# Cross-attention on one core: V's row halves moved behind the transposes, the first pair's scores in two PSUM banks of their own, the last step handled pair by pair

## What is computed

```python
h = _layernorm(x, gamma, beta)                       # x: (8, 256, 256)
Q = (h @ Wq).reshape(B, NQ, N_HEADS, HEAD_DIM)       # 16 heads of 64
K = (context @ Wk).reshape(B, NC, N_HEADS, HEAD_DIM) # context: (8, 256, 192)
V = (context @ Wv).reshape(B, NC, N_HEADS, HEAD_DIM)
attn = jnp.einsum('bihd,bjhd->bhij', Q, K)
attn = jax.nn.softmax(attn, axis=-1) * scale
vals = jnp.einsum('bhij,bjhd->bihd', attn, V).reshape(B, NQ, INNER)
out = vals @ Wo + bo
return x + out
```

## Time and profile before

| | |
|---|---|
| median of three runs | 330.03 us |
| the profiled execution's own time | 329.93 us |
| its span (first to last instruction) | 327.9 us |
| PE busy | 319.3 us, 97% |
| DVE and ACT busy | 253.1 us each, 77% |
| POOL busy | 155.2 us, 47% |
| share of PE in the chain that ended last | 93% |
| granted TensorE clock | full in every slice |

### The profile page before, as it was taken

The page is one execution under the profiler, slowest core; times in us unless marked ns, Lnnn a source line. Parts: engine busy times, 40 slices in busy tenths (PEclk is TensorE's granted clock), DMA queues, the critical chain, the costliest instruction groups (busy, mean ns, idle before and its releaser), DMA issues.

```text
span 327.9 us, 9688 instructions
## 1 busy us (share of the span) xinstructions
PE 319.3 (97%) x3771; PEld 280.9 (86%) x3771; DVE 253.1 (77%) x588; ACT 253.1 (77%) x798; POOL 155.2 (47%) x288
## 2 busy tenths in 40 slices
PE   5999999999999999999999999999999999999985
PEld 4879888899888889988889988889988888988874
DVE  5898787977778788787878778787777878767784
ACT  4899888877878877888777877787787887776862
POOL 5586578616644256433662336631664425233330
PEclk9999999999999999999999999999999999999999
DMA  6980000020001100020000200003000000000000
GB/s 181 262 256 4 0 2 3 2 91 2 2 1 54 37 3 0 2 90 2 3 3 3 88 2 2 2 1 91 2 2 2 32 3 2 2 3 32 2 3 32
DMA packets 10860, 10.70 MB, mean 33 GB/s; under 512 B 960, under 2 KB 10304, under 8 KB 10816
## 3 DMA queue, kind: packets, MB, share of 16 engines
q1 hardware_dynamic: 10336, 9.77, 9.9%
q10 hardware_dynamic: 416, 0.33, 0.3%
q0 software_dynamic: 64, 0.00, 0.1%
HBM read 8.00 MB, written 2.10 MB: 31 GB/s over the span
## 4 chain that ended last, share of the span: by engine, by line
PE 93%; DVE 3%; ACT 2%; POOL 1%; issue 1%; DVEq 0%; POOLq 0%
PE mix_ps L892 18%; PE ring_ps L863 14%; PE ring_ps L958 13%; PE o_ps L1000 13%; PE ring_ps L916 11%; PE ring_ps L1037 9%; PE ring_ps L1077 8%; PE ring_ps L1084 3%; ACT prob L462 1%; PE ring_ps L936 1%; PE mix_ps L834 1%; PE mix_ps L826 1%; PE o_ps L821 1%; DVE prob_t L803 1%; DVE qk_lo L702 1%
## 5 line engine op out<-in xcount | busy, mean ns | idle before, releaser
L371 POOL TENSOR_SCALAR prob<-prob,inv 128x256 f32<-128x256 f32 x192 | 89.7, 484 | 106.6 <-DVE inv L684 106.4
L462 ACT ACTIVATE prob<-ring_ps,neg_max 128x256 f32<-128x256 f32 x256 | 118.1, 475 | 21.6 <-DVE neg_max L677 21.5
L677 DVE TENSOR_REDUCE neg_max<-ring_ps 128x2 f32<-128x512 f32 x128 | 81.4, 679 | 0.4 <-PE ring_ps L863 0.3
L892 PE MATMUL mix_ps<-prob_t,v_sb 128*64 128x256 f32 x504 | 61.5, 386 | 0.5 <-DVE prob_t L803 0.5
L702 DVE TENSOR_TENSOR qk_lo<-ring_ps,qk_hi 128x512 fp32r<-128x512 f32 x64 | 44.2, 691 | 18.0 <-ACT qk_hi L472 18.0
L803 DVE COPY prob_t<-ring_ps 128x512 f32<-128x512 f32 x64 | 41.2, 686 | 21.3 <-PE ring_ps L1037 21.3
L462 ACT ACTIVATION_READ_ACCUMULATOR prob<-ring_ps,neg_max 128x1 f32 x256 | 53.0, 207 | 0.0
L472 ACT ACTIVATE qk_hi<-ring_ps 128x512 fp32r<-128x512 f32 x64 | 38.6, 603 | 13.8 <-PE ring_ps L958 13.8
L892 PEld LDWEIGHTS mix_ps<-prob_t,v_sb 128*64 128x64 f32 x504 | 33.5, 136 | 18.3 <-issue 0.6
L863 PE MATMUL ring_ps<-qk_hi 64*128 64x256 f32 x256 | 39.6, 302 | 0.1
L1037 PE MATMUL ring_ps<-ident,prob 64*128 64x64 f32 x1024 | 37.4, 223 | 0.2 <-DVE prob L692 0.2
(11 more groups left out here) (130 smaller groups left out, 684.8 us busy)
## 6 DMA issues: line engine op xcount, KB each, us to landing
x_in<-in_x_dram SPq DMA_DIRECT2D x8, 256.0 KB, 3.2
out_dram<-y_sb SPq DMA_DIRECT2D x7, 256.0 KB, 2.2
c_in<-in_ctx_dram SPq DMA_DIRECT2D x7, 192.0 KB, 3.0
w_raw<-in_L_xattn_Wq_dram SPq DMA_DIRECT2D x8, 128.0 KB, 3.1
w_raw<-in_L_xattn_Wo_dram SPq DMA_DIRECT2D x4, 256.0 KB, 4.6
w_raw<-in_L_xattn_Wk_dram SPq DMA_DIRECT2D x4, 128.0 KB, 3.5
w_raw<-in_L_xattn_Wk_dram SPq DMA_DIRECT2D x8, 64.0 KB, 3.2
w_raw<-in_L_xattn_Wv_dram SPq DMA_DIRECT2D x2, 256.0 KB, 4.2
```

The costliest lines, as they stand in the source:

```text
L371: last = nc.gpsimd.tensor_scalar(prob[:, e, r, :], prob[:, e, r, :], inv[:, e, r:r + 1], SCALE, ALU.mult, ALU.mult)
L462: last = nc.scalar.activation(prob[:, e, r, :], score_bank(u, e)[:, r * ROWS:(r + 1) * ROWS], ACT.Exp, bias=neg_max[:, e, r:r + 1], accum_ ...
L677: nc.vector.tensor_reduce(neg_max[:, e, :], score_bank(u, e)[:, :].rearrange("p (r j) -> p r j", r=RT), AX, ALU.max, negate=True).then_inc ...
L892: last = nc.tensor.matmul(ps[h * HALF:(h + 1) * HALF, first:first + ROWS], v_sb[:, w // RT % 2, j, p * P + h * HALF:p * P + (h + 1) * HALF ...
```

## The change

- Banks: the first pair's scores and turned probabilities always stand in `ring[2]`; the other two ring pairs alternate (`qk_banks(u)` = `ring[u % 2]`), and the second pair's scores stand in `qk_banks(u)`.
- The waits of `scores(u)` follow: that for the copies of the first pair of step `u - 1` moves ahead of the first pair's scores, that for V's copies moves ahead of the second pair's; each pair waits for its own low parts alone.
- `values_rest(u + 1)`: V's pair of row halves is issued behind `turn(u)`, in steps 2 to 30. ACT's copies of V stand behind its first turned copy.
- Step 31: `mix(30)` puts its second pair into `ring[0][0]`, DVE makes high and low parts pair by pair, `output(30)` waits for each by itself, and the last head is scaled row tile by row tile.

```diff
--- before.py
+++ after.py
@@ -130,17 +130,17 @@
 
         def qk_banks(u):
 
-            return ring[u % 3 if u else 2]
+            return ring[u % 2]
 
         def score_bank(u, e):
 
-            return ring[(u - e // 2) % 3][e % 2]
+            return (ring[2] if e < 2 else qk_banks(u))[e % 2]
 
         def context_bank(b):
 
             return {0: ring[1][0], 1: o_ps}.get(b, mix_ps)
 
-        x_banks = ring[0]
+        x_banks = ring[2]
 
         def part(high, i, c0, c1):
 
@@ -149,6 +149,10 @@
             if i < O0:
                 return (wv_lo, wv_hi)[high][:, i - V0, c0:c1]
             return (wo_lo, wo_hi)[high][:, i - O0, c0:c1]
+
+        def copied(w, a):
+
+            return BATCH * w + a + 1
 
         def turned_half(e):
 
...
@@ -484,8 +493,8 @@
                 if u == STEPS:
 
                     for a in range(BATCH):
-                        act.wait_ge(mixed, u + a)
-                        nc.scalar.activation(mix_hi[:, a, :], (mix_ps, ring[2][0])[a][:, 0:ROWS],
+                        act.wait_ge(mixed, u + 1 + a)
+                        nc.scalar.activation(mix_hi[:, a, :], (mix_ps, ring[0][0])[a][:, 0:ROWS],
                                              ACT.Copy).then_inc(mix_hi_ready, 1)
                 elif 1 <= u < STEPS - 1:
                     act.wait_ge(mixed, u)
@@ -531,26 +540,29 @@
                     if u == 2:
 
                         values_out(2, mix_ps)
-                    if 2 <= u < STEPS - 1:
-                        act.wait_ge(v_made, u + 2)
-                        for k, ps in enumerate(qk_banks(u + 1)):
-                            last = nc.scalar.activation(
-                                v_sb[:, (u + 1) // RT % 2, (u + 1) % RT,
-                                     k * V_HALF:(k + 1) * V_HALF],
-                                ps[:, 0:V_HALF], ACT.Copy)
-                        last.then_inc(v_ready, 1)
+
+                def values_halves():
+                    act.wait_ge(v_made, u + 2)
+                    for k, ps in enumerate(qk_banks(u + 1)):
+                        last = nc.scalar.activation(
+                            v_sb[:, (u + 1) // RT % 2, (u + 1) % RT,
+                                 k * V_HALF:(k + 1) * V_HALF],
+                            ps[:, 0:V_HALF], ACT.Copy)
+                    last.then_inc(v_ready, 1)
 
                 if u != 1:
                     prepared()
                 if 0 <= u < STEPS:
                     if u >= 1:
 
-                        act.wait_ge(mixed, u)
+                        act.wait_ge(mixed, u + (u == STEPS - 1))
                     for e in range(0, HEADS, 2):
                         act.wait_ge(turned, HEADS * u + e + 1)
                         nc.scalar.activation(turned_half(e), score_bank(u, e)[:, :]
                                              .rearrange("p (k i) -> p k i", i=HALF), ACT.Copy)\
                             .then_inc(prob_t_ready[0], 1)
+                        if e == 0 and 2 <= u < STEPS - 1:
+                            values_halves()
                 if u == 0:
                     weight_hi(12)
                     weight_hi(13)
...
@@ -685,10 +697,21 @@
 
                 def last_head():
 
-                    inverse(HEADS - 1)
+                    if u == STEPS - 1:
+                        dve.wait_ge(prob_first, 1)
+                        nc.vector.reciprocal(inv[:, HEADS - 1, 0:1], sums[:, HEADS - 1, 0:1])\
+                            .then_inc(inv_first, 1)
+                        dve.wait_ge(inv_first, 1)
+                        nc.vector.tensor_scalar(prob[:, HEADS - 1, 0, :], prob[:, HEADS - 1, 0, :],
+                                                inv[:, HEADS - 1, 0:1], SCALE, ALU.mult, ALU.mult)
+                        dve.wait_ge(prob_ready, HEADS * u + HEADS)
+                        nc.vector.reciprocal(inv[:, HEADS - 1, 1:2], sums[:, HEADS - 1, 1:2])\
+                            .then_inc(inv_ready, 1)
+                    else:
+                        inverse(HEADS - 1)
                     if 0 <= u < STEPS:
                         dve.wait_ge(inv_ready, HEADS * u + HEADS)
-                        for r in range(RT):
+                        for r in range(1 if u == STEPS - 1 else 0, RT):
                             last = nc.vector.tensor_scalar(prob[:, HEADS - 1, r, :],
                                                            prob[:, HEADS - 1, r, :],
                                                            inv[:, HEADS - 1, r:r + 1], SCALE,
@@ -706,13 +729,23 @@
                                                 ALU.subtract)\
                             .then_inc(qk_lo_ready, 1)
 
+                def mix_hi_pair(a):
+
+                    dve.wait_ge(mixed, u + a)
+                    nc.vector.tensor_copy(mix_hi[:, a, :], (mix_ps, ring[0][0])[a][:, 0:ROWS])\
+                        .then_inc(mix_hi_ready, 1)
+
                 maximum(0)
                 maximum(1)
                 if u == 1:
                     weight_lo(13)
                 maximum(2)
                 inverse(0)
+                if u == STEPS - 1:
+                    mix_hi_pair(0)
                 maximum(3)
+                if u == STEPS - 1:
+                    mix_hi_pair(1)
                 inverse(1)
                 if u == 1:
                     context_lo(1, context_bank(1))
...
@@ -837,9 +867,6 @@
                 last.then_inc(x_turned, 1)
 
             def scores(u):
-
-                if u >= 3:
-                    pe.wait_ge(v_ready, u + 1)
                 for a in range(BATCH):
                     if u == 1 and a == 1:
                         pe.wait_ge(c_loaded[1], 16)
@@ -850,11 +877,14 @@
                         for k in range(BATCH):
                             keys(BATCH + k, k, parts=(1,))
 
-                    pe.wait_ge(qk_lo_ready, BATCH * u + (a + 1 if u == 0 else BATCH))
-                    if u >= 1 and a == 1:
+                    pe.wait_ge(qk_lo_ready, BATCH * u + a + 1)
+                    if u >= 1 and a == 0:
 
                         for h in range(2):
-                            pe.wait_ge(prob_t_ready[h], BATCH * (u - 1) + 1)
+                            pe.wait_ge(prob_t_ready[h], copied(u - 1, 0))
+                    if u >= 3 and a == 1:
+
+                        pe.wait_ge(v_ready, u + 1)
                     passes = ((qk_hi, qk_hi), (qk_hi, qk_lo), (qk_lo, qk_hi))
                     for r in range(RT):
                         for n, (q, key) in enumerate(passes):
...
@@ -882,11 +912,11 @@
                     pe.wait_ge(h_full_ready, DT * b + 1)
                 for a in range(BATCH):
                     for h in range(2):
-                        pe.wait_ge(prob_t_ready[h], BATCH * w + a + 1)
+                        pe.wait_ge(prob_t_ready[h], copied(w, a))
                     p = (BATCH * w + a) % GROUP
 
-                    own_bank = w == STEPS - 1 and a == 1
-                    ps, first = (ring[2][0], 0) if own_bank else (mix_ps, a * ROWS)
+                    own_bank = w >= STEPS - 2 and a == 1
+                    ps, first = (ring[0][0], 0) if own_bank else (mix_ps, a * ROWS)
                     for j in range(RT):
                         for h in range(2):
                             last = nc.tensor.matmul(
...
@@ -975,11 +1005,9 @@
                     pe.wait_ge(y_ready, b)
                 if w == STEPS - 2:
 
-                    pe.wait_ge(mix_hi_ready, w + 1)
                     for m, weights in ((mix_hi, (wo_hi, wo_lo)), (mix_lo, (wo_hi,))):
-                        if m is mix_lo:
-                            pe.wait_ge(mix_lo_ready, w + 1)
                         for a in range(BATCH):
+                            pe.wait_ge(mix_hi_ready if m is mix_hi else mix_lo_ready, w + 1 + a)
                             o, cols = divmod(BATCH * s + a, GROUP)
                             cols = slice(cols * D, (cols + 1) * D)
                             for r in range(RT):
...
@@ -1039,6 +1067,22 @@
                                 prob[own, 2 * a + h, r, j * P:(j + 1) * P], ident[own, own])
                             if k == 2 * RT * RT - 1:
                                 last.then_inc(turned, 1)
+
+            def values_rest(n):
+
+                g, j = divmod(n, RT)
+                b, half = divmod(g, 2)
+                rows = slice(j * P, (j + 1) * P)
+                tiles = c_val if b else c_t
+                first = half * PIECE
+                pe.wait_ge(c_rest_ready, b + 1)
+                high = (c_rest[:, b % 2, rows], tiles[HALF:P, b % 2, 1, rows])
+                for a, ps in enumerate(qk_banks(n)):
+                    own = slice(a * HALF, (a + 1) * HALF)
+                    last = nc.tensor.matmul(ps[:, 0:V_HALF], high[a],
+                                            wv_lo[own, 1, first + a * V_HALF:first + (a + 1) * V_HALF],
+                                            start=False, stop=True, skip_group_check=True)
```

(46 more changed lines are left out.)

2 lines of the change are left out of this document (1 added, 1 removed).

## The result

The changed kernel takes 348.14 us (median of four, 347.5 to 348.62) against 329.93 us (four runs of the kernel before on the same chip): ratio 1.0552, 95% interval 1.0539 to 1.0564. It is slower by 18.2 us, where 13.8 were forecast. The direction and the place of the new wait were right, the size was not, and the time lies above the range.

The account below looks back on a forecast made before the run. PE, busy for 97% of the span, was taken to bound the kernel. 329.93 + 13.3 (29 middle steps) + 0.9 (step 0) - 0.4 (last step) = 343.7, with 0.1 for the median 343.8 us; range 337.5 to 347.

Parts of the forecast that it names:

- What bounds the kernel: PE, busy for 97% of the span and all 9.51 us of a middle step; waits cost one for one.
- The gain of the move: V's pair behind the transposes in a middle step: 1.49 us by starts, a gain of 0.10 a step, not reached.
- The new wait: First pair's scores wait for DVE's turned copy, 28 to 30 times; release 0.14 us, following start 0.22 us.
- The step that failed: Middle steps: second start of the scores at 158.68 against 158.22, +0.46 us a step, times 29 +13.3 us.
- upper sum: Whole kernel with the upper bound for the middle steps: 329.93 + 13.6 + 0.9 = 344.5 us.
- Step 0: Scores of step 1 wait for step 0's copies until 21.04 instead of starting at 20.10: +0.94 us.
- Last step: Step 31: the 0.98 us wait for the wide copy goes, but transposes wait for POOL: -0.4 us.
- V's copies: Ready 0.22 us before the second pair's scores, costing nothing; rival that only V's wait binds: 336.8 us, 3 in 100.
- Granted clock: Stays at 1.00 (2.4 GHz); rival with 1.2 GHz for a tenth of the span: +33 us, near 377, 1 in 100.

Follow-up runs that it names:

- split_turn: Kernel after, in steps 2 to 30 the first pair's transposes ahead of V's full matmuls, the second pair's behind them, V's pair last: 351.45 us, ratio 1.0659.
- rings_only: Kernel after with V's pair of row halves back in front of the transposes and ACT's copies of V ahead of its turned copies: 350.31 us, ratio 1.0620.
- half_copy: Kernel after, from step 2 on the first pair's turned copies take only 256 of 512 columns (output not the reference's): 342.95 us, ratio 1.0398.
- split_rest: split_turn with V's pair of row halves put back directly behind V's full matmuls, ahead of the second pair's transposes: 341.42 us, ratio 1.0354.
- last_tuned: last_only with low parts ahead of head 2's reciprocal and head 1's reciprocal ahead of the second narrow copy: 329.26 us against 329.80, ratio 0.9983.
- move_only: Kernel after with the old ring of three bank pairs and the old order of the waits of scores(u): 357.16 us, ratio 1.0827.
- last_only: Kernel before with the change's edits for step 31 only: 329.87 us against 330.12, ratio 0.9995.
- delay16: Kernel after with a memset of 16 columns ahead of DVE's first copy, from step 2 on: 347.54 us, ratio 1.0536.
- delay112: Kernel after with a memset of 112 columns ahead of DVE's first copy, from step 2 on: 349.60 us, ratio 1.0599.

## Why the prediction was right in kind and wrong in size

- *What bounds the kernel*: right. PE had no hole in a middle step, and every wait came out of the total.
- *The gain of the move*: "a gain of 0.10 us a step", not reached, as said. By the starts it would have been half of that, since the 32 transposes take 1.01 us behind a full matmul (164.90 to 165.91) and not 0.96; split_turn has the 0.20 and 0.12 us behind them (V's pair at 168.05, scores at 168.25 and 168.37). No run has the move without a wait behind it. By rings_only against the kernel after the move gives back 0.12 to 0.17 us a step once the banks are new, because V's pair then fills a part of the wait.
- *The new wait*: right in its place, number and releaser: DVE's copy, 29 times, release 0.15 us (0.14), first scores start 0.20 behind (0.22). rings_only, half_copy and split_rest show it three ways: longer without V's pair behind the transposes, shorter with a shorter copy, gone under other cover wherever DVE is free to copy in time.
- *The step that failed*: "That is +0.46 us a step", with 0.47 as its upper bound. Measured are 17.2 us over 29 steps, 0.59 each. Two pieces were missing. The smaller: I took DVE's copy 0.79 us behind the first transpose, as it stands behind V's pair. Behind a full matmul it is 0.84 (165.74 - 164.90), and 32 transposes take longer to get through there, 1.21 against 1.16 us. The row was among mine: 319.72, 1.21, beside 157.06, 1.16. With it a step at the faster pace should take 9.51 + 0.46 + 0.05 = 10.02 us, which it does. The larger: PE's slower pace in 15 of 28 steps, 0.18 us in nine of them and 0.14 in six, 2.5 us. The prediction had put it at nothing without a word: "keys, queries, output and V of the step" were only moved, at the pace of before. Together 29 x 0.51 + 2.5 = 17.3 us of the 17.2 measured. Smaller things cancel: DVE's copy comes 0.04 us later still in steps 4, 8, ..., 24, where it has the context's low parts to make first, and 0.37 later in step 28; but the kernel before has a wait and the slower pace of its own in steps 28 and 29, 0.67 us. With the smaller piece alone the sum would be 329.93 + 0.89 + 14.8 - 0.2 = 345.4 us, inside the stated range of 337.5 to 347. It is the slower pace that took the time above it. (The prediction's upper sum is 344.4, not 344.5.)
- *Step 0*: right, +0.89 for +0.94. *Last step*: half of the forecast gain; the chain hangs on ACT's exponentials (2.85 us of it in one piece, from 333.38) and not on POOL. last_tuned shows what was to be had.
- *V's copies*: "ready 0.22 us early, and cost nothing as long as the first wait is there" holds in the trace after; split_turn and half_copy show what V's wait does once the first wait is gone or shorter. *Granted clock*: 1.00 throughout, as forecast.

Open is what in a release decides the pace. The distance from the first transpose to the release doesn't: in the kernel after it is 1.69 us in step 9, at 113.3 ns, and in step 10, at 117.7. Nor does the wait alone: rings_only and move_only have 29 such waits each, and of their steps 2 to 29 only one is slow, step 2 of rings_only. That the moment of the release matters is shown by the two delays only in so far as nothing else was changed; one memset also shifts DVE's later work.

## What to carry to other kernels

When buffers are reassigned, list for each wait what lies between its last producer and it, in the new order: here a wait that had 0.27 us to spare cost 0.5 us a step once it stood 0.8 us earlier. Two waits of nearly the same due time have to be priced together, since covering one uncovers the other. Where the bounding engine has run without a hole, count something for its restarts beside the wait itself: its pace after them may differ.

## What was not expected of the hardware

- Full matmuls of 256 columns follow one another every 113.3 or every 117.7 ns, at the same granted clock (1.00). The kernel before keeps the first from step 3 to step 27 and goes over to the second behind the one short wait of step 28's copy, at 294.96. last_only has the same short wait in step 28, at 295.18, and stays at 113.3 ns. rings_only with 29 waits stays at the faster pace in all but one of its steps, and the kernel after falls to the slower in 15. The pace can also go over where PE waits for nothing, as in step 7 of the kernel after, behind the transposes of the context.
- An instruction more on a waited-for engine can leave the kernel no slower: delay16, with 30 memsets more on DVE and releases 0.03 us later in most steps, measured 347.54 against 348.14 us, and the intervals of the two ratios overlap.
- In the kernel before, DVE's first copy of step 28 starts 1.16 us behind the first transpose instead of 0.79, with nothing on DVE ahead of it; in the kernel after the same copy is late by 0.37 us too, in last_only PE also loses 0.33 us in that step. In delay16 and delay112, with the memset ahead of it, the copy of step 28 is no later than that of its neighbours. The cause was not looked for.
